# Moving the transposes of the SwiGLU product behind the next block's first gate-up half

## What is computed

```python
xs = x[tok_sorted]                                  # 4096 tokens x 4 choices, sorted by expert
g = ragged_dot(xs, gate_weight^T, group_sizes)      # 512 -> 256, 32 experts
u = ragged_dot(xs, up_weight^T, group_sizes)        # 512 -> 256
hmid = silu(g) * u
o = ragged_dot(hmid, down_weight^T, group_sizes)    # 256 -> 512
y = zeros.at[tok_sorted].add(o * weight)
```

## Time and profile before

| | |
|---|---|
| median of 3 runs | 3252.62 us (3252.36 to 3259.63) |
| the profiled execution, its own time | 3253.32 us |
| its span | 3251.6 us |
| TensorE busy | 2698.2 us, 83% of the span |
| VectorE busy | 1631.8 us, 50% |
| ScalarE busy | 1306.9 us, 40% |
| GpSimd busy | 1089.8 us, 34% |
| granted TensorE clock, mean over the span | 0.902 |
| weight DMAs `f_wraw<-w_in` | 64 of 1536 KB, 7.2 us median to landing |

### The profile page before, as it was taken

One profiled execution on the slowest core, in us unless ns is written; L12 is line 12 of the kernel. 1 busy time (PEld: TensorE's weight loads), 2 busy tenths in 40 slices (PEclk: granted clock), 3 DMA queues, 4 the chain that ended last, 5 costly groups with the idle time before them and its releaser, 6 DMA issues. The chain is left out here.

```text
span 3251.6 us, 65525 instructions
## 1 busy us (share of the span) xinstructions
PE 2698.2 (83%) x13668; PEld 1963.3 (60%) x13669; DVE 1631.8 (50%) x3136; ACT 1306.9 (40%) x3316; POOL 1089.8 (34%) x1529
## 2 busy tenths in 40 slices
PE   1259999999992799999899999986899999999800
PEld 0148887888881455555555555553788788888700
DVE  8754444544433364654646465542444445454245
ACT  1235555555542222322322232221555555555422
POOL 2435555555541000100110001001455555455456
PEclk9999999999996788888897888886999999999955
DMA  2335444455403344343434434320455455543088
GB/s 71 129 123 173 163 160 154 173 175 173 151 13 116 94 112 118 98 129 93 130 93 122 114 91 127 79 79 36 154 175 172 150 167 173 178 158 110 1 322 298
DMA packets 153904, 434.78 MB, mean 134 GB/s; under 512 B 30993, under 2 KB 32529, under 8 KB 141538
## 3 DMA queue, kind: packets, MB, share of 16 engines
q1 hardware_dynamic: 95520, 282.25, 27.9%
q0 software_dynamic: 55936, 151.10, 13.9%
q10 hardware_dynamic: 2370, 0.64, 0.1%
HBM read 290.10 MB, written 125.83 MB: 128 GB/s over the span
## 5 line engine op out<-in xcount | busy, mean ns | idle before, releaser
L430 PE MATMUL f_psg<-f_wh,f_xh 128*128 x1280 | 563.5, 440 | 17.0 <-DVE f_idle L575 9.1
L430 PE MATMUL f_psg<-f_wh,f_xl 128*128 x1280 | 505.8, 395 | 0.0
L430 PE MATMUL f_psg<-f_wl,f_xh 128*128 x1280 | 504.1, 394 | 0.0
L380 POOL DMA_INDIRECT f_xg<-xn_rows,f_it x320 | 337.4, 1054 | 264.9 <-POOL f_it L377 264.0
L388 POOL DMA_INDIRECT y_rows<-f_ob,f_ip x320 | 329.5, 1030 | 284.6 <-POOL f_ip L385 253.3
L1219 DVE TENSOR_REDUCE a_mx<-a_psa 128x1 f32<-128x128 f32 (+3 forms) x512 | 237.6, 488 | 243.4 <-PE a_psa L983 234.6
L569 DVE TENSOR_TENSOR f_wl<-f_wraw,f_wh 128x768 f32 x256 | 244.9, 959 | 200.0 <-ACT f_wh L494 199.9
L582 DVE TENSOR_TENSOR f_xl<-f_psx,f_xh 128x512 fp32r<-128x512 f32 x320 | 221.0, 691 | 210.7 <-ACT f_xh L505 203.9
L505 ACT ACTIVATE f_xh<-f_psx 128x512 fp32r<-128x512 f32 x320 | 191.3, 598 | 264.4 <-PE f_psx L417 256.2
L1124 ACT ACTIVATE a_pt<-a_psb 128x256 f32<-128x256 f32 (+3 forms) x512 | 208.6, 436 | 193.1 <-PE a_psb L1032 188.4
L430 PEld LDWEIGHTS f_psg<-f_wh,f_xh 128*128 128x128 f32 x1280 | 242.5, 189 | 65.4 <-issue 35.0
(11 more groups left out here) (163 smaller groups left out, 4819.3 us busy)
## 6 DMA issues: line engine op xcount, KB each, us to landing
f_wraw<-w_in SPq DMA_DIRECT2D x64, 1536.0 KB, 7.2
a_y<-y_rows SPq DMA_DIRECT2D x128, 256.0 KB, 3.8
z_y<-y_rows SPq DMA_DIRECT2D x32, 1024.0 KB, 7.2
a_stq<-a_qk SPq DMA_DIRECT2D x128, 192.0 KB
a_stk<-a_qk SPq DMA_DIRECT2D x128, 192.0 KB
r_xt<-x_in SPq DMA_DIRECT2D x32, 256.0 KB, 4.3
xn_rows<-r_xo SPq DMA_DIRECT2D x32, 256.0 KB, 3.0
a_xt<-x_in SPq DMA_DIRECT2D x8, 1024.0 KB, 8.0
```

The lines of the kernel that those rows point to most:

```text
L380: g.indirect_dma_start(xg[:, j, :], None, xn_d, bass.IndirectOffsetOnAxis(it[:, j:j + 1], 0), bounds_check=tok_max, oob_is_err=False).then ...
L430: mm = pe.matmul(psg[:, j, :], x[:, j, k, :], w[:, cols], start=(k == 0 and n == 0), stop=(k == DC - 1 and n == 2))
```

## The change

On TensorE, `turn_h` of a block is taken from the end of its own turn to the middle of the next turn: after the first half of the next block's gate-up, right before that turn's `turn_x`. The read of the slot register is moved from behind `down` to behind `turn_x`; since it now comes before `down` of the block before, four registers take the place of two. On ScalarE `product_high` and on VectorE `product_low` move in the same way: from behind the weight quarters 1 and 3 of their own turn to the start of the next turn, ahead of the row work of the next block, and so behind the weight quarters 0 and 2. No instruction is added or taken away but for one more at the end of a stage's code.

```diff
                 def turn(b, r):
                     j = r % 2
-                    gate_up(b, j, (0, 1))
+                    gate_up(b, j, r, (0, 1))
+                    if not below(b, 1):
+                        turn_h(b - 1, 1 - j)
                     if there(b + 1):
                         turn_x(b + 1, 1 - j)
-                    gate_up(b, j, (2, 3))
+                        find_slot(b + 1, (r + 1) % NS)
+                    gate_up(b, j, r, (2, 3))
                     if not below(b, 1):
-                        down(b - 1, 1 - j)
-                    if there(b + 1):
-                        find_slot(b + 1, 1 - j)
-                    turn_h(b, j)
+                        down(b - 1, 1 - j, (r + 3) % NS)
...
@@ ScalarE
                         find_new(b + 3, (r + 3) % NS)
+                    if not below(b, 1):
+                        product_high(b - 1, 1 - j)
                     if there(b + 1):
                         rows_high(b + 1, 1 - j)
                     silu(b, j)
...
                         result(b - 1, 1 - j)
-                    product_high(b, j)
                     if there(b + 3):
                         weights_high(b + 3, (r + 3) % NS, 0)
...
@@ VectorE
                         find_new(b + 3, (r + 3) % NS)
+                    if not below(b, 1):
+                        product_low(b - 1, 1 - j)
                     if there(b + 1):
                         rows_low(b + 1, 1 - j)
                     product(b, j)
...
                         weights_low(b + 1, (r + 1) % NS, 3)
-                    product_low(b, j)
                     if there(b + 3):
                         weights_low(b + 3, (r + 3) % NS, 0)
```

More of the change, by code:

```diff
@@ L418, in turn_x, with gate_up @@
                     mm.then_inc(s_xt, 1)
-                def gate_up(b, j, chunks):
-                    at = pe.snap(slot[j], min_val=0, max_val=TOP)
+                def gate_up(b, j, r, chunks):
+                    at = pe.snap(slot[r], min_val=0, max_val=TOP)
                     if chunks[0] == 0:
@@ L433, in gate_up, with down @@
                         mm.then_inc(s_gu, 1)
-                def down(b, j):
-                    at = pe.snap(slot[j], min_val=0, max_val=TOP)
+                def down(b, j, r):
+                    at = pe.snap(slot[r], min_val=0, max_val=TOP)
                     pe.wait_ge(s_wd, b + 1)
@@ L454, in turn_h, with find_slot @@
                     mm.then_inc(s_ht, 1)
-                slot = [pe.alloc_register(f"{name}_slot{j}") for j in range(2)]
-                def find_slot(b, j):
-                    pe.reg_load(slot[j], blk[0:1, 2, ds(b, 1)])
+                slot = [pe.alloc_register(f"{name}_slot{r}") for r in range(NS)]
+                def find_slot(b, r):
+                    pe.reg_load(slot[r], blk[0:1, 2, ds(b, 1)])
                 def turn(b, r):
                     j = r % 2
-                    gate_up(b, j, (0, 1))
+                    gate_up(b, j, r, (0, 1))
+                    if not below(b, 1):
+                        turn_h(b - 1, 1 - j)
                     if there(b + 1):
                         turn_x(b + 1, 1 - j)
-                    gate_up(b, j, (2, 3))
+                        find_slot(b + 1, (r + 1) % NS)
+                    gate_up(b, j, r, (2, 3))
                     if not below(b, 1):
-                        down(b - 1, 1 - j)
-                    if there(b + 1):
-                        find_slot(b + 1, 1 - j)
-                    turn_h(b, j)
+                        down(b - 1, 1 - j, (r + 3) % NS)
                 turn_x(0, 0)
@@ L475, in _ @@
                 blocks(pe, turn)
-                down(NB - 1, 1)
+                turn_h(NB - 1, 1)
+                down(NB - 1, 1, (NB - 1) % NS)
             @block.scalar
@@ L553, in _ @@
                 blocks(a, turn)
+                product_high(NB - 1, 1)
                 result(NB - 1, 1)
@@ L619, in _ @@
                 blocks(v, turn)
+                product_low(NB - 1, 1)
 def attend(nc, tb, d):
```

## The result

The changed kernel takes 3264.86 us (median of 8 runs, 3261.15 to 3266.83), the kernel before in the same comparison 3252.49 us (8 runs). The ratio is 1.0033, 95% interval 1.0022 to 1.0044: some 11 us slower by the ratio and 12 by the medians, clear of no change, and close to the 3260 that were forecast. The profiled execution took 3263.98 us at a span of 3262.3 us and a clock of 0.904.

The account below looks back on a forecast made before the run. TensorE, busy 789 of 819 and 820 us in the two expert stages, was taken as the bound. Loop ends -36, first turns -2 and weight turns +46 gave +8 us: 3260 us, own range 3250 to 3272.

Parts of the forecast that it names:

- The gap at the loop end: TensorE at the expert stages' loop ends: all of the 0.47 us lost per loop body goes, 76 times, 36 us less.
- rival 3: At TensorE's loop ends: the branch opens a gap however far ahead the queue is, 27 us stay, 3287 us; chance 0.07.
- The first turns: First turn of each expert stage: the second block's matmuls fill TensorE's 0.93 us wait for the first product, 2 us less.
- Six transposes together: On TensorE: transposes cost in proportion to their number, so one group less saves 0; at most 26 us otherwise.
- The register load: Slot register load before the second gate-up half: hidden by TensorE's queue being some 2 us ahead, cost 0.
- rival 4: The slot's register load shows on TensorE: 320 x 0.38 = 122 us more, 3382 us; chance 0.02.
- The weight turns: Turns with quarter 0 or 2 of new weights: late `f_hl` makes TensorE wait before `down`, 46 us more.
- Rival 1: In the weight turns: the copies fit and little of the 46 us is left, 3215 us with none; chance 0.22.
- Rival 2: Weight turns' chain 0.15 us longer: 19 us more, 3279 us; chance 0.27 with the forecast's upper part.
- the first term: The loop-end gain on TensorE, 36 us less, first in the sum -36 - 2 + 46.

Follow-up runs that it names:

- before_u8: The kernel before with a loop body of 8 turns instead of 4, so 19 loops a stage instead of 38: 3238.27 us, ratio 0.9964 to the kernel before.
- split: The changed kernel with the two product transposes three matmuls ahead of the row transposes instead of together with them: 3262.74 us, ratio 1.0043 to the kernel before.
- noload: The changed kernel with VectorE's load of the flag for block b+3 behind product instead of ahead of product_low: 3244.99 us, ratio 0.9982 to the kernel before.
- fix: The changed kernel with VectorE's weight quarters 0 and 2 moved behind the next turn's product_low, the flag's load behind product: 3227.87 us, ratio 0.9933 to the kernel before.

## Why the prediction was right, point by point

- *The gap at the loop end* was a late queue. It goes when the wait on the product stands half a turn earlier than the branch (7 idle loads of the gate-up instead of 76), and halves with the number of loop ends when it stands there (before_u8). This rules out rival 3, a gap that stays. The size was off: 29 us by the medians, 31 by the sum over all turns, instead of 36. I took one loop body of 19.75 us and a floor of 19.28; the medians are 19.69 and, for the joined transposes, 19.31.
- *The first turns* brought 4.3 us net instead of 2, and what is above the forecast is luck. From the last gate-up matmul to the next turn, where the idle 0.93 us stood, the two stages took 2.3 us less, 1.9 net of the moved transposes: as forecast. The rest is the clock. Two matmuls of the first turn's second gate-up half, before and after:

```profile
205.19 0.63 PE L430 MATMUL f_psg<-f_wh,f_xl 128*128 x1
205.62 0.63 PE L430 MATMUL f_psg<-f_wh,f_xh 128*128 x1
```

```profile
204.94 0.40 PE L430 MATMUL f_psg<-f_wh,f_xl 128*128 x1
205.18 0.39 PE L430 MATMUL f_psg<-f_wh,f_xh 128*128 x1
```

  Their starts are 0.43 us apart before and 0.24 after: the granted clock rose from the 1.2 to the 2.4 GHz level 5.8 and 6.2 us after the two stages' first matmuls before, 3.2 and 3.0 us after them in the changed kernel's profile. With the matmuls around it that made 2.4 us in both stages. TensorE does the same in both kernels up to the rise, and in before_u8, with the old order, the rise came after 5.3 and 3.1 us, so no run shows the change moving it.
- *Six transposes together* save nothing: right, by split.
- *The register load* in the middle of the turn costs nothing, so rival 4 is out. Between row transposes and gate-up no gap is added: a plain turn would show it and takes 4.83 us.
- *The weight turns* were the main term, 46 us forecast for 124 turns and 49 measured for 120 (50 for all 124). The chain from the last matmul of `down` over result copy, high part, low part and `product_low` back to `down` held step by step. Medians for quarter 0 in the loop body, from the turn's first matmul, with the forecast behind: weight copy 0.77 (0.70), `f_wl` 1.94 (1.89), end of `f_hl` 3.43 (3.39), and `down`'s second matmul 0.53 behind it (0.54). For quarter 2: 0.95 (0.85), 2.14 (2.02), 3.43 (3.33). So the copies start some 0.1 us later than taken, which makes quarter 2 too low by 0.06. Quarter 2 behind loop ends was too high by 0.10, because its step from `f_wl` to `f_hl` is 1.08 us and not 1.17. That the flag's load makes quarter 0 and the loop ends dear was argued from two distances and is shown by noload; that `product_low`'s place is the cause is shown by fix.
- *Three turns outside the chain.* Quarter 0 in the loop body has a median wait of 0.30 us but a mean of 0.34. Three turns with quarter 0, one in the body and two behind a loop end, waited 1.40, 1.50 and 1.11 us. In each, ScalarE's result copy had first waited 1.4, 2.8 and 2.0 us for an earlier scatter, once the raw weights too (0.81 us), and the weight copy and all behind it were late. The sums of ScalarE's waits for a scatter (us, times, longest), changed kernel and kernel before:

```profile
ACT f_ob L519 <- DMA y_rows<-f_ob,f_ip: 20.2, 21, 2.8
```

```profile
ACT f_ob L518 <- DMA y_rows<-f_ob,f_ip: 2.8, 1, 2.8
```

  They came 14 times in before_u8, so they are not the change's alone; but there no wait before `down` was longer than 0.4 us. The three turns add some 2 us to the 49.
- *Rival 1* (the copies fit) is out by fix, which would have gained nothing. *Rival 2* (the weight turns cost more) is the direction in which the forecast missed, by 3 us of 46, some 2 of them from the three turns above; the first term missed by 5 to 7 the same way and the first turns by 2 the other, which is the clock's luck and makes the sum look better than its terms. The time lies 5 us above the forecast. The ratio 1.0033 is just beyond the bound of 0.3% that divides "same" from "slower", where the chances were 0.42 and 0.36, and its interval has the bound inside.

The rule on control flow of the Trainium skill ("Advanced Engine Details and Errata", Control Flow Timing, about 108 ns for a compare-and-branch) would have made the loop ends worth 8 us; before_u8 shows 0.33 us a loop end, three times as much. The branch is only a part of what stands open there: in the trace of the kernel before, TensorE's compare-and-branch at the loop end of the earlier trace rows starts at 619.53 and lasts 0.21 us, and four short instructions of the queue follow before the weight load at 620.25.

## What to carry to other kernels

When work moves on the bounding engine, follow it on the helpers as well: here the product's low part fell behind weight copies that had stood at the end of a turn because nobody waited for them there. Count the cover in the turns that do extra work, not in the usual ones, and put the rare long copy ahead of the result with the most cover. An idle load marked "issue" ahead of a loop's first matmul can be a sign of a wait standing just before the branch, as here; moving that wait gave the time back, and a longer loop body half of it.

## What was not expected of the hardware

A queue that had run dry cost twice in these traces. In fix the gate-up began 0.11 us late for the late operand, and its second matmul followed after 0.33 us instead of 0.23. The same step of 0.33 us (347.92 to 348.25) stands in each of the 125 turns of the changed kernel in which `down` had to wait, and 0.23 in the others. The queue's records in fix show what stood behind the wait: the short instructions for the second matmul are recorded from 287.37 to 287.63, behind the weight load at 287.34 that was waited for, and the matmul comes at 287.68. That they are what makes the step longer was not tested.
